# Key, value and receptance products in three rounded parts, sums by transfers, and a new order in a hybrid RWKV, mixture-of-experts and gated-recurrence kernel

## What is computed

```
xn = layer_norm(x); lx = time_shift(xn)
k = (xn*mix_k + lx*(1-mix_k)) @ w_key        # 256 x 256, also v and r with their own mixes
sr = sigmoid(r);  w = exp(time_decay)
# over t, for each of 256 columns (numerically stable):
#   out_t = (e1*alpha + e2*v_t) / (e1*beta + e2),  e1 = exp(eps-tau), e2 = exp(u+k_t-tau)
#   alpha = d1*alpha + d2*v_t; beta = d1*beta + d2; eps = max(eps-w, k_t)
x = x + (out * sr) @ w_output
# channel mix: relu(.. @ f_w_key)**2 @ f_w_value, gated by sigmoid(.. @ f_w_recept)
```

## Time and profile before

| | |
|---|---|
| median of 3 runs | 1257.09 us (1254.84 to 1258.42) |
| span of the profiled execution, first to last instruction | 1254.1 us |
| PE busy | 1186.7 us, 95% |
| DVE busy | 886.8 us, 71% |
| ACT busy | 699.7 us, 56% |
| POOL busy | 537.4 us, 43% |

### The profile page before, as it was taken

The page is one execution under the profiler, slowest core; times in us unless marked ns, Lnnn a source line. Parts: engine busy times, 40 slices in busy tenths (PEclk is TensorE's granted clock), DMA queues, the critical chain, the costliest instruction groups (busy, mean ns, idle before and its releaser), DMA issues. The chain is left out here.

```text
span 1254.1 us, 17087 instructions
## 1 busy us (share of the span) xinstructions
PE 1186.7 (95%) x5812; PEld 927.7 (74%) x5812; DVE 886.8 (71%) x1508; ACT 699.7 (56%) x1100; POOL 537.4 (43%) x514
## 2 busy tenths in 40 slices
PE   5699999999999999999999989999999999999982
PEld 2377787887776868778786768778778678688871
DVE  7989886757587757677889898678567655654336
ACT  2464463555554637455568677567676464554633
POOL 3537652435153062443478637436353602253024
PEclk9799999999999999999999999999999999999997
DMA  7012154646458267575331045657555554656534
GB/s 211 17 34 51 13 164 134 186 122 191 158 138 240 73 162 212 157 202 163 92 85 34 1 105 154 186 158 180 139 146 159 167 167 144 198 140 200 141 100 127
DMA packets 113030, 170.78 MB, mean 136 GB/s; under 512 B 10024, under 2 KB 86576, under 8 KB 112944
## 3 DMA queue, kind: packets, MB, share of 16 engines
q1 hardware_dynamic: 94864, 124.59, 31.2%
q0 software_dynamic: 12320, 39.86, 16.0%
q10 hardware_dynamic: 5760, 5.25, 1.2%
HBM read 138.20 MB, written 16.27 MB: 123 GB/s over the span
## 5 line engine op out<-in xcount | busy, mean ns | idle before, releaser
L2248 PE MATMUL psum<-fwv,hid 128*128 128x256 f32 x1024 | 239.9, 380 | 2.6 <-ACT hid L1225 2.6
L786 POOL TENSOR_TENSOR rstd<-varis,half_neg 128x4 f32<-128x4 f32 x64 | 101.2, 1580 | 282.4 <-DVE varis L3169 191.8
L2248 PEld LDWEIGHTS psum<-fwv,hid 128*128 128x128 f32 x1024 | 190.0, 190 | 32.6 <-issue 4.6
L2289 PEld LDWEIGHTS psum<-xst,ew 128*128 128x128 f32 x1024 | 123.9, 192 | 7.5 <-issue 3.1
L2289 PE MATMUL psum<-xst,ew 128*128 128x128 f32 x1024 | 124.8, 275 | 0.5 <-ACT xst L1306 0.5
L1319 ACT ACTIVATE hidt<-psum 128x512 f32<-128x512 f32 x80 | 47.7, 597 | 133.4 <-PE psum L2289 118.1
L2297 PE MATMUL psum<-ew,hidt 128*128 128x256 f32 x512 | 116.0, 379 | 2.6 <-DMA ew<-in_w 1.9
L1221 ACT ACTIVATE hid<-psum 128x512 f32<-128x512 f32 x128 | 75.5, 593 | 62.4 <-PE psum L2169 40.5
L2297 PEld LDWEIGHTS psum<-ew,hidt 128*128 128x128 f32 x512 | 96.5, 190 | 18.6 <-ACT hidt L1319 2.9
L790 POOL TENSOR_SCALAR xhat<-rows_ring,negmean,rstd 128x256 f32<-128x256 f32 x108 | 96.5, 903 | 24.6 <-PE psum L2158 17.9
L2169 PE MATMUL psum<-xfk_hi,fwk_hi 128*128 128x512 f32 x256 | 93.7, 447 | 1.8 <-issue 1.8
(11 more groups left out here) (303 smaller groups left out, 2496.3 us busy)
## 6 DMA issues: line engine op xcount, KB each, us to landing
ew<-in_w SPq DMA_DIRECT2D x64, 1024.0 KB
ew<-in_w SPq DMA_DIRECT2D x64, 512.0 KB
rows_ring<-bias_rows POOLq DMA_DIRECT2D x28, 512.0 KB, 5.6
rows_ring<-in_x SPq DMA_DIRECT2D x14, 512.0 KB, 6.2
rows_ring<-y POOLq DMA_DIRECT2D x14, 512.0 KB, 5.6
out<-rows_ring SPq DMA_DIRECT2D x14, 512.0 KB, 6.5
rows_ring<-space POOLq DMA_DIRECT2D x12, 512.0 KB
ys_rows<-ys ACTq DMA_DIRECT2D x40, 128.0 KB
```

The lines of the kernel that those rows point to most:

```text
L786: pool.tensor_tensor(dst, src, half_neg[:, 0:src.shape[1]], ALU.pow).then_inc(done, 1)
L2248: last = nc.tensor.matmul(rows4[:, k, :], hid[:, j % NHID, k * P:(k + 1) * P], fwv[:, j, :], start=j == 0 and k % 2 == 0, stop=j == FC - 1 ...
L2289: last = nc.tensor.matmul(bank_e[:, j * P:(j + 1) * P], ew1[:, c, at:at + P], xst[:, c, :], start=c == 0, stop=c == DC - 1)
```

## The change

1. The key, value and receptance products of batches 1 to 15 go through `columns_split`. The three weights are loaded into the scratch tile `space`, and split once into `kw` (high part by ACT, rest by DVE). Each batch's mixes are split too: ACT copies a rounded high part (128 x 1024) into the place of `top`, `beta` or `alpha`, DVE subtracts it from the mix, in place. Batch 0 keeps the float32 products, from `space`.
2. The arguments of the scan's exponentials come from one surplus, `kc - decay' - top` (decay' is the stored negative decay), which takes the place of the old `top`; then `weights_now` is one operation per half, and the decays are a maximum and a minimum with zero over both halves.
3. For batches 0 to 14 `combine` is an adding transfer from POOL's queue, and so is `merge_bias`; batch 15 keeps the sum on DVE.
4. Some buffers move: `xfr` now lies in `xhat[1]`, which makes `norm2` and `rows_mid` wait for the previous batch's `receptances`; `hid_rows[0]` lies in a half of `hidt`; the recurrence of position 14 uses `y` for its normed rows.
5. All five lists have a new order. ACT's has 18 more table loads.

```diff
-        xfr = sb("xfr", [P, DC, T])
+        xfr = xhat[1][:].rearrange("p c d -> p (c d)").rearrange("p (c n) -> p c n", c=DC)
+        kw = [sb(f"kw_{part}", [P, 3, DC, D], F32R) for part in ("hi", "lo")]
...
+            def columns_of(dst, b, n, m, whole, parts):
+                if b:
+                    columns_split(dst, [w[:, n] for w in kw], m, parts, kvr)
+                else:
+                    columns(dst, kvr_whole[:, n], m, whole, kvr)
...
-                pe.wait_ge(mix1.sem, mix1.count(b, "k1"))
+                if b:
+                    pe.wait_ge(key_lo.sem, key_lo.count(b - 1, "lo"))
...
+            def split_kvr_high():
+                act.wait_ge(kvr_loaded, 3 * 16)
+                nc.scalar.activation(kw[0][:], kvr_whole, ACT.Copy).then_inc(kvr_split_hi, 1)
+            def high_of_key(b):
+                act.wait_ge(mix1.sem, mix1.count(b, "k1"))
+                nc.scalar.activation(key_parts[0], xk, ACT.Copy).then_inc(key_hi.sem, 1)
...
+            def low_of(whole, parts, hi, lo, b):
+                dve.wait_ge(hi.sem, hi.count(b - 1, "hi"))
+                nc.vector.tensor_tensor(parts[1], whole, parts[0].bitcast(F32), ALU.subtract).then_inc(lo.sem, 1)
...
             def weights_ahead(b):
+                dve.wait_ge(kvr.sem, kvr.count(b, "k1"))
+                nc.vector.memset(top[:, :, 0:1], -1e30).then_inc(tops.sem, 1)
...
+            def surpluses(b):
...
+                    nc.vector.scalar_tensor_tensor(top[:, c, 0:T], kc[:, c, :], decay[:, c:c + 1], top[:, c, 0:T],
+                                                   ALU.subtract, ALU.subtract).then_inc(surplus.sem, 1)
             def weights_now(b):
...
-                    nc.vector.scalar_tensor_tensor(g[:, c, :], kc[:, c, :], col("first", c), was[:, c, :],
-                                                   ALU.add, ALU.subtract).then_inc(weight_now.sem, 1)
-                nc.vector.tensor_scalar(g[:], g[:], LOGIT_CAP, None, ALU.min).then_inc(weight_now.sem, 1)
+                    nc.vector.tensor_scalar(g[:, c, :], top[:, c, 0:T], ahead[:, c:c + 1], LOGIT_CAP, ALU.add, ALU.min)\
...
             def weights_decayed(b):
-                    nc.vector.scalar_tensor_tensor(dec[:, 0, c, :], was[:, c, :], decay[:, c:c + 1], top[:, c, 1:T + 1],
-                                                   ALU.add, ALU.subtract).then_inc(decays_in.sem, 1)
+                nc.vector.tensor_scalar(dec[:, 0], top[:, :, 0:T], 0.0, -1.0, ALU.max, ALU.mult).then_inc(decays_in.sem, 1)
...
-                nc.vector.tensor_tensor(dec[:, 1], kc[:], top[:, :, 1:T + 1], ALU.subtract).then_inc(decays_in.sem, 1)
+                nc.vector.tensor_scalar(dec[:, 1], top[:, :, 0:T], 0.0, None, ALU.min).then_inc(decays_in.sem, 1)
...
+            def combine(b):
+                pool.wait_ge(comb.sem, comb.count(b, "g"))
+                pool.wait_ge(plus_z.sem, plus_z.count(b, "z"))
+                pool.dma_start(rows_of(b).rearrange("p c d -> p (c d)"), sf[:].rearrange("p c d -> p (c d)"), accum_op=ALU.add)\
+                    .then_inc(summed.sem, 16)
+            def merge_bias(f, b):
+                pool.wait_ge(experts_hat.sem, experts_hat.count(f, f"h{NCH - 1}"))
...
             def norm2(b):
...
+                await_step(pool, fr, b - 1, "f")
```

Of the new order, the part of turn 3 on POOL and on PE that the prediction speaks of (before, then after, up to the first expert tile):

```diff
             def turn_3():
-                norm_power(0)
                 keep2(2)
-                gather(0)
-                gather(1)
+                combine(1)
                 keep1(3)
+                norm_power(0)
+                gather(0)
                 norm1(4)
...
             def turn_3():
                 channel_key(2, 0)
                 channel_key(2, 1)
                 channel_key(2, 2)
-                channel_key(2, 3)
                 channel_value(2, 0)
-                channel_key(2, 4)
-                channel_key(2, 5, -1)
                 channel_value(2, 1)
+                channel_value(2, 2)
+                channel_key(2, 3)
+                channel_key(2, 4)
+                channel_key(2, 5, -1)
+                channel_key(2, 6, -1)
                 receptances(2)
                 tile_in(0)
```

2366 lines of the change are left out of this document (1268 added, 1098 removed).

## The result

The changed kernel took 1273.54 us in the median (1270.85 to 1275.38), the kernel before 1256.37 beside it: a ratio of 1.0134 with a 95% interval of 1.0115 to 1.0153, 16.8 us more where the forecast had 13 less. One of the ten executions of `a_free` was in a slow state (2439 us) and is left out.

What follows compares the result with a forecast made beforehand. PE was taken to bound turns with expert tiles, DVE or nearly so the middle. Span 1254.1 - 19.1 (products) + 1 (middle) + 5 (first tile) = 1241.0 us; with 3.0 from span to median, 1244 us, own range 1236 to 1252.

Steps and rivals of the forecast that it cites:

- DVE's early turns, worked out at 97%: Turns without tiles or recurrence: DVE's 44.07 + 1.45 = 45.5 us must fit into 46.9, so PE's gain there is not realised.
- Products, work: Key, value and receptance products: 90 outputs at 1.3975 us instead of 1.715, 28.6 us less PE work.
- rival 4: Split products at three quarters of the float32 time, 0.43 us less an output, 26 instead of 19.1, 1237 us; chance 0.03.
- Products, realised: PE's 1.9 us a batch counted in full for 10 batches, 19.1 us; five early and middle batches counted as nothing.
- The early and middle turns, written off: PE's gain of batches 1 to 3, 10 and 11 counted as not realised, 5 x 1.9 = 9.5 us.
- Path to the keys: Copy and subtraction between mix and keys, 2.3 us, some 4.5 with queued operations; covered by other PE work, costed at nothing.
- Sums by transfers: Sums on POOL's queue make rows ready 5.3 us later, hidden everywhere but at the first experts; costed at nothing elsewhere.
- a lock-out of the size that I had weighed: DVE's two-port operations blocking POOL's 19 transfer issues: 19 x 0.72 = 14 us of POOL if each waited; left out of the sum.
- First expert tile: Turn 3: gather 5.3 to 14 us later, PE idling 0 to 11 us before the tile's transposes; 5 taken.
- The term of 1 us for the middle: Middle turns, where DVE's 58.35 us exceed the turn's 58.20, get longer by 0 to 3 us; 1 taken.
- Rival 2: Splits stand bare before the keys, 4.5 us in ten of fifteen batches, first tile 5: 1278 us, slower; chance 0.12.
- Rival 3: DVE bounds six early and middle batches, each 1.45 us longer instead of 1.9 shorter, first tile 5: 1254 us; chance 0.20.

Runs made afterwards that it cites:

- a_free: `a_order` with split-form products reading rounded mixes in place of both parts, no copies or subtractions, sums on DVE: 1256.9 us, 0.9998 against before.
- a_order: The changed kernel's order with the work of before: single float32 products, no mix copies or subtractions, sums of batches 0 to 14 on DVE: 1267.4 us, 1.0098.
- a_nosplit: The changed kernel without the 45 copies on ACT and 45 subtractions on DVE, rounded mixes read in place of both parts: 1262.0 us, 1.0059.
- a_nolow: The changed kernel without the 45 subtractions on DVE; ACT's copies stay and products read the high part three times: 1264.0 us, 1.0055.
- a_sum_dve: The changed kernel with the sums of batches 0 to 14 as DVE additions again; bias transfers stay: 1278.4 us, 1.0190.
- b_free: The kernel before, own order, with key, value and receptance products of batches 1 to 15 as three products of one rounded operand, nothing split: 1242.5 us, 0.9884.
- b_split: `b_free` with the 45 copies and 45 subtractions put into before's lists, each at the first place after its operand: 1279.8 us, 1.0185.
- b_one: `b_free` with one rounded product in place of three for keys, values and receptances of batches 1 to 15: 1242.1 us, 0.9889.

## Why the prediction was wrong

The forecast was some 30 us too low, and no single term has it all. The largest part are the steps that it put at nothing: that DVE's early turns, worked out at 97%, take the subtractions and only fail to shrink, and that the sums' landing "is hidden everywhere but at the first experts". The subtractions cost 9.9 us and the sums 7.7. The products gave 6.5 less than counted, and the order took 6.3 more. The runs lead from before to after in these steps (ratios times 1256; a line is uncertain by some 3 us):

| step | forecast | measured |
|---|---|---|
| order with its 18 table loads, moved buffers, surplus, split of the weights, bias by transfer (before to `a_order`) | +6 | +12.3 |
| products (`a_order` to `a_free`) | -19.1 | -12.6 |
| sums by transfers (`a_free` to `a_nosplit`) | 0 | +7.7 |
| copies on ACT (`a_nosplit` to `a_nolow`) | 0 | -0.5 |
| subtractions on DVE (`a_nolow` to after) | 0 | +9.9 |
| together | -13 | +16.8 |

The way through the runs is one of several; another order of steps splits the sum otherwise, as `a_sum_dve` shows.

- **Products, work.** Right. The outputs that begin at 1163.14 and 1164.54, six records each, start 1.40 us apart, the 1.3975 of the sum. "FP8 and Floating Point Precision" of the Trainium skill (TensorE Precision Notes) gives true float32 four passes; the estimated 1.29, which takes one pass for the rounded form, does not fit, and rival 4 with it.
- **Products, realised.** The term that was mis-sized: 19.1, and 12.6 to 14.6 in three backgrounds. The step that failed is "a microsecond saved on PE shortens a turn with tiles by as much". A window in which PE is busy from end to end shows that nothing was late, not by how much it was early. In `b_free` the nine turns with tiles between the keys of batches 4 and 9 and of 11 and 15 gave 8.8 us of the 17.1 counted. Part of the rest is the clock (last section). The early and middle turns, written off, gave 4 us.
- **Path to the keys, and room on DVE.** PE waits 1.6 us for the subtractions: right about the path. But I asked who waits for the subtraction, and not what stands behind it on DVE. The 9.9 us come in the main from the early turns, which I had at 97% and counted as not shrinking: they grew. The later turns did have the room, as a sum (1.6 us over eleven of them, `a_nolow` against the changed kernel). Which step behind the subtractions PE then waited for is not shown one by one; between 60 and 200 us its wait for `channel_value`'s squares is the longest, 3.69 us against 2.2 in `a_nolow`.
- **Sums by transfers.** The landing was sized right (6.3 us in the median); that "recurrences follow their batch by one or more turns" is wrong for batch 14, whose values and statistics stand in one turn with four steps between them, and PE waited 4.59 us there. That ACT needs `sf` back before the next batch was not in the sum at all. These are the places found; that they make up the 7.7 us is not shown. As to the Trainium skill's "SBUF — State Buffer" (Who interferes with whom): the 15 issues took 0.84 to 1.22 us, so a lock-out of the size that I had weighed is not seen there.
- **First expert tile.** The chain was right and the price was luck. The gather came 11.9 us later, and the tile's transposes 9.7, but PE had other work and idled for 1.35 us in front of them, not 5:

```profile
176.82 1.20 POOL L927 DMA_INDIRECT xs<-xf_rows,token_of_slot  x1 [9.55 <-DMA xf_rows<-ew]
182.40 0.44 PE L2423 MATMUL psum<-ident,xs 128*128 128x128 f32 x2 [1.35 <-DMA xs<-xf_rows,token_of_slot]
```

Up to 200 us the stalls grew by 11.2, where early turns and tile together had been forecast at 11; but nearly all of it lies ahead of the tile.

- **Order.** The term of 1 us for the middle was too small. The window between the keys of batches 10 and 11, which was to show DVE at 97%, reads:

```profile
666.54:739.40 72.86, 65.87 (x301) 53.77 (x300) 63.91 (x108) 56.31 (x86) 41.76 (x37) 0.98 0.20 43
```

It is 14.7 us longer than in the earlier trace rows and holds 10 us more of PE's work, so turns cannot be compared across the two orders, and DVE is at 88%. The 12 us of the order are shown as a sum (`a_order`); of their parts only the moved buffer was tried, and it is not seen among them. The 18 table loads (23 us of ACT) were not tried alone, nor was the order without them, so what in the order costs stays open.

Rival 2 had the time nearest (1278 us) and its mechanism shows in `b_split`, but not in the changed kernel, whose order hides the way to the keys. Rival 3, DVE as the bound more widely, had the engine and, for the early turns, the place right; its 1254 us were 20 short, since it has neither the sums, nor the order, nor the half of the products that turns with tiles do not give. Neither of the signs by which the prediction wanted to be proved wrong came: the early and middle turns did not shrink like the others, and PE's waits in front of the new products stayed small.

## What to carry to other kernels

An engine that is busy from end to end says that its work bounds the kernel now, not how far: before counting a saving in full, ask how early its inputs were, or shorten it in a run that costs nothing and see where the gain stops. A step added to an engine that runs its list in order costs by its place: price what stands behind it, turn by turn, and the buffer that it holds, not its share of the busy time; here nearly all of the subtractions were free and those in the crowded early turns were not. In a kernel whose lists were fitted to one set of durations, as here, two engines can stand level, and then a change that relieves one by loading the other gives part of the one and pays for the other.

## What the runs showed of the hardware that I had not expected

PE's busy time fell by less than its work: by 19.2 us of 28.6 in `b_free`, by 59 of 83.5 from `b_free` to `b_one`, by 13.2 of 28.6 in the changed kernel. The mean granted clock goes with it: 0.986 before, 0.977, 0.957, 0.975. In the changed kernel PE stood idle for 2.02 us before 640.98; soon after, the granted clock is at the lower of its two levels (1.2 GHz, elsewhere 2.4):

```profile
641.50:644.90 3.40, 3.40 (x13) 2.81 (x12) 3.26 (x4) 2.78 (x5) 3.40 (x3) 0.50 0.00 0
```

There the records of the split form start 0.43 us apart, and 0.23 on either side. Summed over all stretches at 0.50, PE is busy for 12 us before, 28 in `b_free`, 36 in the changed kernel and 67 in `b_one`. Half of that, 6, 14, 18 and 33 us, is my estimate of what the lower clock took: 8 us more than before in `b_free`, 12 in the changed kernel, 19 from `b_free` to `b_one`. So part of a gain on PE that turns into waits is lost a second time, to slower products; how much of it reaches the kernel's time is not shown.
